# A fused two-layer block on one core: the last mixture of experts computed only for the two experts chosen per token, on rows sorted by expert in DRAM

## The reference, cut to what matters

```python
gate_scores = jax.nn.softmax(jnp.einsum('btd,ed->bte', x, Wg), axis=-1)
topk_val, topk_idx = jax.lax.top_k(gate_scores, TOP_K)          # TOP_K = 2
topk_val = topk_val / (topk_val.sum(axis=-1, keepdims=True) + EPS)
comb = (jax.nn.one_hot(topk_idx, E, dtype=x.dtype) * topk_val[..., None]).sum(axis=-2)
for e in range(E):                                              # E = 8
    h = jnp.einsum('btd,hd->bth', x, W1[e]) + b1[e]             # 128 -> 512
    a, b = jnp.split(h, 2, axis=-1)
    g = a * jax.nn.sigmoid(b)
    out = out + (jnp.einsum('bth,dh->btd', g, Wo) + bo) * comb[..., e:e + 1]
```

## Time and profile before

| | |
|---|---|
| median of 3 runs | 639.04 us (635.58 to 644.13) |
| the profiled execution, its span | 656.7 us |
| stage C, from the first transposes of `z` to the end | 295.8 to 656.7 us |
| first logits / logits of the last batch | 319.5 / 610.0 us |
| busy: PE, DVE, POOL, ACT | 85%, 71%, 66%, 46% |

### The profile page before, as it was taken

One profiled execution on the slowest core, in us unless ns is written; L12 is line 12 of the kernel. 1 busy time (PEld: TensorE's weight loads), 2 busy tenths in 40 slices (PEclk: granted clock), 3 DMA queues, 4 the chain that ended last, 5 costly groups with the idle time before them and its releaser, 6 DMA issues.

```text
span 656.7 us, 10345 instructions
## 1 busy us (share of the span) xinstructions
PE 560.0 (85%) x3181; PEld 457.0 (70%) x3181; DVE 469.3 (71%) x1573; ACT 304.8 (46%) x825; POOL 433.9 (66%) x478
## 2 busy tenths in 40 slices
PE   5978888699337868888898998989989899899993
PEld 4767777555226656677687886878968789788772
DVE  1568788689949423477677879877897888887873
ACT  2657765449201111125364735646456464464440
POOL 6454443319574566538887998988889899653673
PEclk9999998989555555599999999989999999799997
DMA  4697666559320121142330030300403000000000
GB/s 129 168 330 279 244 241 247 225 137 236 76 67 28 45 61 50 34 163 106 125 129 1 12 134 8 137 1 9 137 9 116 21 10 9 0 17 1 8 9 16
DMA packets 47225, 62.04 MB, mean 94 GB/s; under 512 B 13026, under 2 KB 39873, under 8 KB 46146
## 3 DMA queue, kind: packets, MB, share of 16 engines
q1 hardware_dynamic: 44610, 56.15, 26.8%
q0 software_dynamic: 2560, 5.23, 2.8%
HBM read 35.16 MB, written 24.13 MB: 90 GB/s over the span
## 4 chain that ended last, share of the span: by engine, by line
PE 48%; DVE 19%; issue 5%; POOL 5%; another core or an unknown queue 3%; DMA 2%; ACT 2%; POOLq 0%; SPq 0%; DVEq 0%
PE pair L1424 8%; PE pair L1425 8%; PE pair L1426 8%; PE pair L1757 5%; PE pair L1536 2%; DVE cand L1953 2%; DVE c_g L1222 2%; PE pair L1634 2%; PE pair L1767 2%; POOL c_acc L934 2%; DVE keyT L1955 2%; PE pair L1541 2%; POOL c_rs_a L921 1%; PE pair L2063 1%
## 5 line engine op out<-in xcount | busy, mean ns | idle before, releaser
L934 POOL TENSOR_TENSOR c_acc<-c_acc,c_g 128x512 f32<-128x512 f32 x112 | 144.4, 1290 | 39.9 <-DVE c_g L1222 32.9
L1070 ACT ACTIVATE c_sg<-pair 128x256 f32<-128x256 f32 x256 | 95.4, 386 | 94.7 <-PE pair L1426 92.1
L1424 PE MATMUL pair<-c_w_hi,c_x3h 128*128 128x512 f32 x256 | 111.1, 434 | 14.1 <-DVE c_g L1222 13.1
L1222 DVE SCALAR_TENSOR_TENSOR c_g<-pair,c_comb,c_sg 128x256 f32<-128x256 f32 x224 | 100.6, 478 | 26.2 <-ACT c_sg L1070 21.1
L1426 PE MATMUL pair<-c_w_hi,c_x3l 128*128 128x512 f32 x256 | 102.7, 401 | 0.0
L1425 PE MATMUL pair<-c_w_lo,c_x3h 128*128 128x512 f32 x256 | 102.6, 401 | 0.0
L1424 PEld LDWEIGHTS pair<-c_w_hi,c_x3h 128*128 128x128 f32 x256 | 49.4, 193 | 25.7 <-DVE c_g L1222 16.0
L1426 PEld LDWEIGHTS pair<-c_w_hi,c_x3l 128*128 128x128 f32 x256 | 49.2, 192 | 11.8
L1425 PEld LDWEIGHTS pair<-c_w_lo,c_x3h 128*128 128x128 f32 x256 | 49.5, 193 | 8.2
L1835 POOL DMA_INDIRECT routed_rows<-x1T_all,dest_row x32 | 31.7, 992 | 30.6 <-DVE x1T_all L1747 21.4
L1830 POOL DMA_INDIRECT rows_all<-token_rows,tok_row x32 | 31.3, 977 | 14.8 <-issue 9.4
(11 more groups left out here) (374 smaller groups left out, 1478.8 us busy)
## 6 DMA issues: line engine op xcount, KB each, us to landing
routed_rows<-rows_all SPq DMA_DIRECT2D x8, 2048.0 KB
c_c<-routed_rows SPq DMA_DIRECT2D x7, 2048.0 KB, 8.2
token_rows<-a_xw SPq DMA_DIRECT2D x8, 384.0 KB, 2.8
a_x<-in_L_attn_x SPq DMA_DIRECT2D x8, 256.0 KB, 3.5
base_all<-a_xw SPq DMA_DIRECT2D x8, 256.0 KB, 3.2
c_c<-routed_rows SPq DMA_DIRECT2D x4, 512.0 KB, 5.3
out<-c_outb SPq DMA_DIRECT2D x16, 128.0 KB, 1.8
wgu_late<-in_L_ffn_w_gate SPq DMA_DIRECT2D x4, 480.0 KB, 7.6
```

Source lines behind the costliest of these rows:

```text
L934: g.tensor_tensor(acc, acc, b["g"][:, (2 * uf + i) % 4, :, :], ALU.add).then_inc(s["acc"], 1)
L1070: a_.activation(b[f"sg{q % 2}"][:, x, :], self.pair[q % 2][:, x, H1:2 * H1], SIG).then_inc(s["sig"], 1)
L1222: v.scalar_tensor_tensor(out=dst, in0=self.pair[q % 2][:, x, 0:H1], scalar=b[f"comb{uf}"][:, j * E1 + e:j * E1 + e + 1], in1=b[f"sg{q % 2} ...
L1424: t.matmul(dst, w_hi, x_hi, start=start, stop=False)
```

## The change

The seven expert passes over all eight experts go. After the routing of batch n, each token's row (128 values, its weight, the index of its result row: 130 words) is written twice to DRAM, at the next free slot of each of its two experts' regions (`expert_rows`, 8192 slots per expert). PE finds the slots by products with a triangular matrix and a matrix of ones (`ranks`), DVE reads them and forms weights and slots (`read_ranks`, `dispatch`), and POOL writes the rows with 8 indirect DMAs of 128 rows per batch (`scatter_rows`). Four times (after batches 2, 4, 6 and 7) DVE makes a list of tiles of 128 full slots (`make_list`); after the last, unfilled slots are padded. The tile count is fixed: 36 pairs of tiles, 72 tiles, for the 64 that 8192 rows fill.

A step `step(i)` treats one pair at each of four depths: PE transposes the rows of pair i, multiplies pair i-1 by the weights of its experts, whose numbers PE loads from the list into registers, transposes the gated products of pair i-2, and multiplies pair i-3 by `Wo`; POOL scatters the rows of pair i-3 by the index in the row (`expert_out`). Steps 0 to 15 stand in the attention passes of batches 4 to 7, at slots 1, 5, 10 and 13. Steps 16 to 38 come after the attention of all batches. SP loads the row number of every tile into a register and issues its DMA. At the end, for each batch, two result rows per token are read, added with x3 and the bias (`base_rows`, matmuls with the identity), normed and stored.

In the attention, x3, x2 and the normed input are made by ACT, the first sum of the routed rows (2048 columns) moves from POOL to DVE, the logits are one plain matmul per tile, and x2 is added on PE.

```diff
-AT = dict(zT=0, accT=(8, 1), out=(9, 2), gate=2, y4=(10, 3), quads=3, gate2=3, v=4, outb=(15, 5), kT=5, sim=6, off=7, atd=6, av=8, w=9, x3=10, x3T=12, lg=13, y=7, z=11)
+AT = dict(zT=0, rank=1, gate=2, quads=3, gate2=3, v=4, kT=5, sim=6, off=7, atd=6, av=8, w=9, x3=10, x3T=12, lg=13, y=7, z=11)
+NPAIRS = B * 4 + 4
+RING = 8
+LISTS = (2, 4, 6, 7)
+STEP_AT = (1, 5, 10, 13)
+FIRST_STEP_PASS = 4
...
     def sync(self, sp):
...
+        def load_pair(m):
+            n = list_of(m)
+            sp.wait_ge(s["listed"], LISTS.index(n) + 1)
+            for u in range(2):
+                sp.wait_ge(self.dispatched[u], 128 * ((n + 2 - u) // 2))
...
+            for x in range(2):
+                i = 2 * m + x
+                row = sp.value_load(b["rowU"][0:1, i:i + 1], min_val=0, max_val=E1 * ES - P)
+                sp.dma_start(b["xs"][:, m % RING, x, :], self.rows[bass.ds(row, P), :]).then_inc(self.xs_loaded[m % RING][0], 16)
...
     def pool(self, pool):
...
+        for p in range(B):
+            r, at = p + 1, list(steps_of(p).values())
+            if r < B:
+                sums(r)
+            if p:
+                scatter_rows(p - 1, range(0, 2))
+            dest_rows(p)
+            for i in at[0:1]:
+                step(i)
+            if r < B:
+                z_scales(r)
+            for i in at[1:2]:
+                step(i)
+            rstd_a(p)
+            if r < B:
+                x2_scales(r)
+            if p:
+                scatter_rows(p - 1, range(2, NT))
...
+        step(TAIL_STEP)
+        scatter_rows(B - 1, range(NT))
+        for i in range(TAIL_STEP + 1, NPAIRS + 3):
+            step(i)
...
     def act(self, act):
...
+        def step(i):
+            m = i
+            if m < NPAIRS:
+                act.wait_ge(s["xT_mm"], EP + m + 1)
...
+                a_.copy(b[f"xh{m % 2}"][0:P - 1, :], bank[2][0:P - 1, 0:2 * P]).then_inc(s["xh"], 1)
+            m = i - 2
+            if 0 <= m < NPAIRS:
+                act.wait_ge(s["gT_mm"], m + 1)
...
+                a_.copy(b[f"gT{m % 2}"][:, :], bank[3][:, :]).then_inc(s["gT"], 1)
+            m = i - 1
+            if 0 <= m < NPAIRS:
+                for x in range(2):
+                    act.wait_ge(s["u_mm"], EP + 2 * m + x + 1)
...
+                    a_.activation(b["sg"][:, x, :], self.pair[0][:, x, H1:2 * H1], SIG).then_inc(s["sig"], 1)
...
     def dve(self, dve):
...
+                if q == AT["rank"]:
+                    read_ranks(a - 1)
+                    if a + 1 < B:
+                        first_sum(a + 1)
...
+                if q == AT["kT"]:
+                    dispatch(a - 1)
...
     def pe(self, pe):
...
+        def step(i):
...
+            m = i - 1
+            if 0 <= m < NPAIRS:
+                pe.wait_ge(s["listed"], LISTS.index(list_of(m)) + 1)
+                e2 = [pe.value_load(b["expU"][0:1, 2 * m + x:2 * m + x + 1], min_val=0, max_val=E1 - 1) for x in range(2)]
+                pe.wait_ge(s["xl"], m + 1)
+                for x in range(2):
+                    if m >= 1:
+                        pe.wait_ge(s["g"], EP + 2 * (m - 1) + x + 1)
...
+                    split3(self.pair[0][:, x, :], b[f"xh{m % 2}"][:, tok], b[f"xl{m % 2}"][:, tok], w_hi, w_lo).then_inc(s["u_mm"], 1)
```

More of the change, by code:

```diff
@@ L1072, in body @@
-        def body(act, ur, ua, r=None, a=None, f=None, t=None):
-            if first(r):
-                return
-            if first(a):
-                first_pass(r, ur, ua)
-                return
-            uf = ur
-            for q in range(2 * E1):
-                if f is not None:
-                    sig(f, q)
-                if a is not None and q == AT["gate"]:
+            make_z(1)
+            make_x3(0, bank[4])
+            keep_x3T(0)
+            make_x2(1)
+            scores(0)
@@ L1083, in body @@
+        first_pass()
+        for a in range(1, B):
+            steps = steps_of(a)
+            for q in range(16):
+                if q == AT["gate"]:
                     act.wait_ge(s["gate_mm"], 3 * a + 1)
                     gate(a, 0, X)
-                for n, half in ((f, 0), (t, 1)):
-                    if n is not None and q == place("accT", half, a):
-                        act.wait_ge(s["accT_mm"], 2 * n + (half + 1))
-                        a_.copy(b["accT"][:, :], bank[4][:, :]).then_inc(s["accT"], 1)
@@ new lines, in act @@
+                if q == AT["x3"]:
+                    make_x3(a, X)
+                if q == AT["z"] and a + 1 < B:
+                    make_z(a + 1)
+                if q == AT["x3T"]:
+                    keep_x3T(a)
+                    if a + 1 < B:
+                        make_x2(a + 1)
+                if q == AT["lg"]:
+                    scores(a)
+                if q in steps:
+                    step(steps[q])
+        for i in range(TAIL_STEP, NPAIRS + 3):
+            step(i)
@@ L1560, in body @@
[L1560 to L1571 removed]
+            logits(0)
+        first_pass()
+        for a in range(1, B):
+            steps = steps_of(a)
+            for q in range(16):
+                if q in steps:
+                    step(steps[q])
+                if q == AT["zT"]:
@@ new lines, in pe @@
+                if q == AT["x3T"]:
+                    x3_transposes(a)
+                if q == AT["lg"]:
+                    logits(a)
+        step(TAIL_STEP)
+        ranks(B - 1)
+        for i in range(TAIL_STEP + 1, NPAIRS + 3):
+            step(i)
+        pe.wait_ge(s["rank_read"], B)
+        pe.wait_ge(s["ys"], EP + NPAIRS)
+        pe.wait_ge(s["fbase"], B + B)
+        for n in range(B):
+            t.matmul(self.fin_bank(n)[:, :], ident[:, :], self.base_all[:, n, :], start=True, stop=False, skip_group_check=True)
```

1178 lines of the change are left out of this document (658 added, 520 removed).

## The result

The changed kernel takes 744.33 us (743.23 to 745.49, 4 runs) where the kernel before takes 640.64 (635.58 to 644.13, 4 runs): ratio 1.168, 95% interval 1.164 to 1.173, slower. The forecast was 740 us, with a range of 675 to 810.

A forecast was written before the change was run, and what follows sets the result against it. The prediction took a chain of waits across engines, not expert units, to bound each pass. Passes plus 5.5 us, behind the last logits plus 94.5, first pass plus 1: plus 101 on the median 639, so 740 us, range 675 to 810.

The forecast's parts named there:

- likeliest case: Whole kernel: passes of 36 and 45 us, tail steps of 4.2; 740 us, own range 695 to 780, chance 0.60.
- The chain's terms: Pass without experts: engine work laid end to end from logits to next logits, 33.3 us at the full clock.
- The clock: Passes without units: 33.3 us at full clock, up to 40.3 by the skill's rule at low clock; 36 taken.
- Steps in the passes: Passes 4 to 7: four steps each make 45 us; waits for rows add 3 in pass 4, 5 in pass 6.
- The tail's step: One step behind the last logits: 4.2 us, from a 3.7 loop and 3.9 of PE work, with hand-overs.
- the loop: Tail step: products, transposes, drain, copy, sigmoid and DVE's product before the one bank pair is free again, 3.7 us.
- PE's own work: Step: products 1.48, transposes 0.41, Wo product as much, transposes 0.2, two register loads of 0.7; 3.9 us on PE.
- Behind the last logits: Tail: 28 us up to the steady steps, seventeen steps 71, draining 5, end 37; 141 against 46.7, plus 94.5.
- First pass: First pass: its x3l of 0.7 us goes and the 2048-column sum of 2.3 comes, plus 1.
- low clock and dear loads: Passes and tail: passes at 40.3 and 51 us, tail steps at 6, 808 us; chance 0.16.
- shorter passes: Passes: chain overlaps, passes of 28 and 36 us, same tail, 672 us; chance 0.14.
- faster: Passes and tail: expert work was the bound, passes of 24 and 32 us, steps of 3.2, 616 us; chance 0.10.

The follow-up runs named there:

- no_steps: Changed kernel without all 39 steps of the chosen experts and the loads of their rows; 613.58 us, ratio 0.960 to the kernel before.
- bare_passes: no_steps also without ranks, reading them, weights and slots, writes of rows and padding, and lists; 589.21 us, ratio 0.923 to the kernel before.
- filled_passes: Changed kernel with 54 matmuls that nobody reads put into PE's waits in each of passes 1 to 3; 734.56 us, ratio 1.152.
- first_sum_later: Changed kernel with DVE's sum over 2048 columns moved behind the first two gate products; 746.79 us, ratio 1.171.
- changed_again: The changed kernel once more, unedited, as base for the runs of its call; 745.02 us, ratio 1.164 to the kernel before.
- first_step_later: Changed kernel with the first two steps of passes 4 to 7 at slots 4 and 7, not 1 and 5; 736.79 us, ratio 1.155.
- tail_three: Changed kernel with sigmoids ahead of the copy, two PSUM bank pairs from pair 19 on, and padding written one pair earlier; 723.99 us, ratio 1.132.
- two_pairs: Changed kernel with products alternating between two PSUM bank pairs from pair 19 on; 762.0 us, one run, where the kernel before took 658.96.

## Why the prediction was right, step by step

**What bounds a pass** (likeliest case: the chain, not the expert units): right, and shown for the changed kernel: no_steps keeps passes of 35.2 us with no expert work, bare_passes 33.9. Passes 1 to 3 came to 34.4, 35.5 and 35.7 against 36. The kernel before without its units did not run, and its attention differs in places (where x3 and the sums are made, and the clock), so what the old units themselves added to a pass is bracketed by 41.5 less 35.2 and 41.5 less 33.9, 6 to 8 us, and not measured.

**The chain's terms.** I had 33.3 us at the full clock (the terms as written add up to 33.1); the second pass of filled_passes took 33.4, at a clock of 0.90. The terms inside were less good, and that they meet is in part luck. The sum over 2048 columns lasts the forecast 2.3 us, but is not on the path: first_sum_later gained nothing, since PE makes ranks and gate products beside it. In its place the chain has two things that I had not counted: the routing arithmetic ends 1.0 us later (5.7 us behind the start of the logits for 4.7), most of it because the logits run at the low clock (DVE's first maximum starts 1.93 us behind them, and 1.10 in filled_passes), and DVE waits 1.4 us for the ranks. These errors cancel. What the sorting adds to a pass is 1.3 us where I had 2.4, and `dispatch` alone lasts 1.3 where I had 2.2.

**The clock.** I added 2.7 us a pass and gave up to 7. The granted clock is 0.76 of full speed on average in these passes, since it goes between the two levels of 2.4 and 1.2 GHz, and filling PE gains 1.8 us a pass at 0.90; what the full clock would bring was not reached. The Trainium skill ("TensorE: Matmul & The Clock Gate", HAM oscillation) describes a stream of products broken by long waits whose clock falls at each of them. Here it does fall in every pass, to 0.50 (as from 372.1 to 386.1 us), but the time does not go to the upper end that I had worked out by that rule: 34.4 to 35.7 us and not 40.3. I take it that most slow products lie beside another engine's work; only for the sum on DVE is that shown. Where a step stands right ahead of the logits, the low clock costs the pass 2.4 us, as pass 7 shows.

**Steps in the passes.** Between no_steps and changed_again, the sixteen steps and their waits cost 11.0, 11.5, 12.4 and 5.7 us, 40.7 in all; forecast were 4 x 9 and 8 for the waits, 44. The waits of 5.9 and 2.5 us were foreseen at their places; first_step_later shows 4.1 and 1.6 of them on the path. I had the larger one in pass 6 and it is in pass 4. The passes took 289.5 in all against 296.

**The tail's step.** It is 3.84 against 4.2, and the loop that I had at 3.7 is what bounds it: right. Mis-sized was PE's own work, 3.9. Two of its terms are wrong in opposite directions. The two register loads, for which I took 1.4, are 1.16 us when PE has just waited and 0.14 in the steady step. The product with `Wo` is eight matmuls a pair and not four: 0.89 us (from 652.75 to 653.64 in the step of tail_three) where I took 0.41. PE needs 2.94. So the bound is the loop alone, and either the sigmoids ahead of the copy or a second bank pair takes the step to 2.94, a thing that by my sum could hardly gain. The Trainium skill ("DMA: Bandwidth & Descriptors", Latency and other measured facts) states a floor of about 600 ns for a `tensor_load`. Uncovered, one is 0.58 us here, which agrees.

**Behind the last logits.** Up to step 19 it is 23.2 us (28 forecast), seventeen steps take 75.2 (71), the draining 8.8 (5), the end 41.5 (37): 148.7 against 141. The steps would be 65 at 3.84, less than my 71; the other 10 us, which I had not counted, come from PE's 6.35 us wait for rows and from two steps that run partly at the low clock, the one behind the wait (6.77 us) and one near the start (5.73). I had not seen that SP's eight padding writes, issued 1.06 us apart, stand ahead of the load of pair 23. In the draining POOL's scatters, 1.28 us apart, end at 704.66, 4.0 us behind ACT's last copy. At the end there are two output buffers, and ACT waits 8.0 us in all for stores; whether more buffers would shorten the end was not tried. PE's wait for the first rows read back and the longest of ACT's waits are these:

```profile
709.98 1.13 PE L1892 MATMUL pair<-c_c,ident 128*128 128x512 f32 x2 [2.11 <-DMA c_c<-expert_out]
...
721.87 1.65 ACT L1292 ACTIVATE c_outb<-c_c,c_nm_f,c_rs_f 128x128 f32<-128x128 f32 x4 [3.06 <-DMA out<-c_outb]
```

**First pass.** From `z` to the logits it is 27.05 us for 23.72: plus 3.3, where I had 1; in changed_again it is 26.2. I have no cause for the rest.

**The sum.** From the first transposes of `z` on, it is 465.2 us against 360.9: plus 104.3, forecast 101; by the medians plus 103.7. The mechanism came as forecast, but that the sum is so near is in part luck: the passes came 6.5 us below the forecast, what follows them 7.7 above it. The rivals: low clock and dear loads fail on both prices, with passes of 34.4 to 35.7 and a step of 3.84; shorter passes fail with the same passes; faster fails with no_steps, whose passes are 35.2 without any steps.

## What to carry to other kernels

Before work is removed from a pipeline, take away the unit and ask what is left: here a chain of 34 to 35 us stands under a pass of 41.5, so even all of the experts' work in a pass was worth only 6 to 8 us, and everything that the new scheme could only do after the last routing came on top. Work that needs all of the data first (sorted lists, padding) stands behind the passes, where no attention work is left to cover it. In such a tail, look at the loop over each shared buffer first, and only then at instruction counts: a second PSUM pair or another order of two instructions on ACT took 0.9 us off a step of 3.84, the register loads that looked dear 0.14.

## What the hardware showed beyond that

- A register load costs PE 0.58 us after an idle stretch and 0.07 while its array has queued work.
- On one chip ACT stood still for 1 to 5 us before single instructions in the tail, in four kernels, and DVE stood in the same way ahead of `c_goT` in their passes (in two_pairs it starts at 596.71, with PE's products done at 594.1). No other trace has it. The cause is open, and it hid the gain of the shorter step. A kernel that is compared on a time should run beside its own base.
- The same instructions can meet another clock in another execution: pass 7 took 41.6 us in the changed kernel and 44.4 in first_sum_later, 2.4 of it in one step.
- A stream of matmuls that nobody reads, put into PE's gaps, is worth its trouble: 54 per pass took the clock from 0.75 to 0.90 and the pass from 35.2 us to 33.4.
